# Second-layer weights of four experts kept on chip, in an attention and mixture-of-experts block on one Trainium2 core

## The reference

```python
x = x + tanh(g_xattn[0]) * xattn(layernorm(x), ctx_1024, ...)   # 16 heads of 64, rope on k, clip at 11, softmax over 1024
x = x + tanh(g_ffn[0])   * ffn(layernorm(x), w1, b1, w2, b2, wr, br)

def ffn(x, w1, b1, w2, b2, wr, br):        # 4 experts, w1 256x1024, w2 1024x256, the best 2 for each token
    logits = xf @ wr + br
    topk_vals, topk_idx = top_k(logits, 2)
    gates = softmax(topk_vals)
    h = gelu(einsum('nd,edh->enh', xf, w1) + b1[:, None, :])
    y = einsum('enh,ehd->end', h, w2) + b2[:, None, :]
    c = einsum('eh,ehd->ed', gelu(b1), w2) + b2
    out = sum over the 2 of gates * (y_sel - c_sel + c.sum(axis=0))
```

## Time and profile before

| | |
|---|---|
| median of 3 runs | 1188.68 us (1185.8 to 1188.8) |
| the profiled execution | 1186.63 us |
| its span, first to last instruction | 1184.6 us |
| attention, to the start of the expert phase | about 892 us |
| expert phase, 19 tiles | about 278 us, 892.2 to 1170 |
| last sums and stores | about 15 us |
| mean granted clock | 0.977 |

### The profile page before, as it was taken

The page is one execution under the profiler, slowest core; times in us unless marked ns, Lnnn a source line. Parts: engine busy times, 40 slices in busy tenths (PEclk is TensorE's granted clock), DMA queues, the critical chain, the costliest instruction groups (busy, mean ns, idle before and its releaser), DMA issues.

```text
span 1184.6 us, 22834 instructions
## 1 busy us (share of the span) xinstructions
PE 1084.6 (92%) x7853; PEld 721.2 (61%) x7853; DVE 1049.0 (89%) x1831; ACT 686.5 (58%) x1325; POOL 597.5 (50%) x570
## 2 busy tenths in 40 slices
PE   5799999999899999999999999989789987888995
PEld 3555555655555555655555555646438987888984
DVE  6698999899789999988999988799887889999996
ACT  4555556654455765544566555445356775777772
POOL 6332476343337634333764444247644636665672
PEclk9899999999999999999999999999899999999998
DMA  6100010000000100000000003201218545676654
GB/s 175 35 10 11 19 35 21 10 10 10 12 19 24 32 10 10 10 12 19 24 23 11 19 10 116 77 29 55 91 57 276 194 135 172 206 236 216 226 168 144
DMA packets 74752, 87.89 MB, mean 74 GB/s; under 512 B 11771, under 2 KB 67719, under 8 KB 74632
## 3 DMA queue, kind: packets, MB, share of 16 engines
q1 hardware_dynamic: 71256, 77.82, 21.0%
q0 software_dynamic: 3360, 8.53, 2.0%
q10 hardware_dynamic: 16, 0.00, 0.0%
HBM read 70.57 MB, written 16.54 MB: 74 GB/s over the span
## 4 chain that ended last, share of the span: by engine, by line
PE 62%; DVE 20%; issue 7%; POOL 5%; ACT 4%; DMA 1%; SPq 1%; DVEq 0%; POOLq 0%; ACTq 0%
PE pv L1773 14%; PE sc L1759 13%; PE kv L1704 5%; PE kv L1706 4%; PE kv L1705 4%; DVE acc L1129 4%; PE tr L1745 3%; PE mi L1704 2%; PE mi L1706 2%; PE mi L1705 2%; PE sc L1704 2%; DVE big L1544 2%; PE sc L1706 2%; PE sc L1705 2%; DVE q_hid L1602 2%
## 5 line engine op out<-in xcount | busy, mean ns | idle before, releaser
L899 ACT ACTIVATE prob<-sc 128x1024 f32<-128x1024 f32 x256 | 249.5, 1029 | 223.6 <-PE sc L1759 218.7
L679 POOL TENSOR_TENSOR rot_s<-k_raw,sinb 128x256 f32<-128x256 f32 x128 | 107.3, 839 | 365.7 <-ACT k_raw L845 365.6
L1773 PE MATMUL pv<-prob,val 128*32 128x512 f32 x2048 | 247.7, 601 | 4.6 <-DVE prob L1114 4.6
L1114 DVE TENSOR_SCALAR prob<-prob 128x1024 f32<-128x1024 f32 x256 | 183.0, 728 | 43.4 <-ACT prob L899 36.5
L1759 PE MATMUL sc<-q_hid,big 64*128 64x512 f32 x1536 | 215.1, 412 | 4.7 <-issue 4.7
L1129 DVE TENSOR_TENSOR acc<-acc,prob 128x1024 f32<-128x1024 f32 x128 | 205.2, 1624 | 0.0
L1759 PEld LDWEIGHTS sc<-q_hid,big 64*128 64x128 f32 x1536 | 136.2, 186 | 108.2 <-issue 62.2
L683 POOL TENSOR_TENSOR rot_c<-rot_c,rot_s 128x256 f32<-128x256 f32 x128 | 133.5, 1043 | 45.7 <-DVE rot_c L1103 30.9
L1773 PEld LDWEIGHTS pv<-prob,val 128*32 128x32 f32 x2048 | 56.8, 110 | 115.0 <-issue 90.3
L1704 PE MATMUL sc<-big,q_hid 128*128 128x256 f32 x304 | 92.9, 306 | 30.2 <-DVE q_hid L1602 29.5
L1704 PE MATMUL kv<-big,acts 128*128 128x512 f32 x256 | 115.0, 449 | 5.8 <-DVE rot_c L1103 4.4
(11 more groups left out here) (267 smaller groups left out, 2491.1 us busy)
## 6 DMA issues: line engine op xcount, KB each, us to landing
val<-in_L_ffn_w SPq DMA_DIRECT2D x18, 1024.0 KB, 5.4
prob<-in_L_ffn_w SPq DMA_DIRECT2D x18, 1024.0 KB
slots_x<-lat_r SPq DMA_DIRECT2D x1, 5016.0 KB, 17.9
rows<-slots_x SPq DMA_DIRECT2D x19, 264.0 KB
rows<-in_ctx SPq DMA_DIRECT2D x32, 128.0 KB, 2.1
w_raw<-in_L_xattn_Wq SPq DMA_DIRECT2D x16, 256.0 KB, 2.7
w_raw<-in_L_xattn_Wo SPq DMA_DIRECT2D x64, 64.0 KB
acc<-in_L_ffn_w SPq DMA_DIRECT2D x16, 256.0 KB, 2.7
```

Of the source, the lines that this page charges most:

```text
L679: g.tensor_tensor(rot_s[:].rearrange("p (h a c) -> p h a c", h=4, a=2), kh[:, :, ::-1, :], sinb[:, t].unsqueeze(1).to_broadcast([P, 4, 2, ...
L899: a.activation(prob[:, s % 2, i, :], sc[i][:], ACT.Exp, scale=DH ** -0.5).then_inc(exp_done[i], 1)
L1114: v.tensor_scalar(prob[:, s % 2, i, :], prob[:, s % 2, i, :], EXP_LOW, EXP_HIGH, ALU.max, ALU.min).then_inc(clamped[i], 1)
L1773: last = mm(pv[g * 32:(g + 1) * 32, :], val[:, u % 2, 2 * c + i, at:at + 32], prob[:, s % 2, i, h * N:(h + 1) * N], start=c == 0 and i == ...
```

## The change: what it does, and the diff

1. `w2all` (128 KB for each partition) takes the place of `big`. It holds the split second-layer weights of all four experts. During attention the same memory holds the attention's weights and keys, so the split can begin only in the last unit: ten pieces of 1024 columns (2 of w_1 for tile 0, 8 of w_2) instead of four. POOL makes the low parts of pieces 0, 2, 3, 5, 6 and 8, DVE those of 1, 4, 7 and 9. Three raw buffers are used in turn, the third (`temp`) being DVE's scratch memory for the routing.
2. Each tile fetches only w_1 (1 MB). ACT makes four high parts of 512 columns, at m = 0, 2, 4 and 6, and POOL all four low parts. DVE makes none. One semaphore, `w_low`, is raised after the fourth. The late scatters stand after POOL's second chunk, the scatter of results after the third.
3. PE reads the expert's number itself at the start of each tile (`pe.value_load`) and addresses the second-layer weights by register.
4. The attention loop is written out (a Python `for`), on all engines.
5. The split w_1 of odd tiles lies in pieces of `q_hid`, `wq` and `acts`. The last two of these are read by the attention's last products, so the first low parts for tile 1 wait for `q_mm`, the third for `wo_mm`, the last projection. That projection is moved: both its halves stand at n = 4 (before n = 5 and n = 8), the second half into the bank `tr`. The loads of w_1 for tiles 1 and 2 go to `prob` and wait for the last denominators.

```diff
-        big = [sb(f"big{i}", [4 * KT * 1024], F32R) for i in range(2)]
-        wkv = big[0][:].rearrange("p (l k n) -> p l k n", l=2, k=KT)
-        kst = big[1][:].rearrange("p (u j l s) -> p u j l s", u=2, j=2, l=2)
+        w2all = sb("w2all", [E * 2 * MT * D], F32R)
+        wkv = w2all[:, 0:4 * KT * 1024].rearrange("p (l k n) -> p l k n", l=2, k=KT)
+        kst = w2all[:, 4 * KT * 1024:].rearrange("p (u j l s) -> p u j l s", u=2, j=2, l=2)
...
-        PIECE_AT = (3, 4, 6, 7)
-        PIECES = 4
+        ROUNDS_AT = ((), (), (0, 1), (2,), (3, 4), (5,), (6, 7), (8, 9))
+        POOL_PIECES = (0, 2, 3, 5, 6, 8)
+        DVE_PIECES = (1, 4, 7, 9)
+        PIECES = KT + 2 * E
...
+        def w1_of(job, k, part):
+
+            if job % 2 == 0:
+                return acts[:, (part * KT + k) * 1024:(part * KT + k + 1) * 1024]
+            if part == 0:
+                return q_hid[:, 4 * N + k * 1024:4 * N + (k + 1) * 1024]
+            return (wq[:].rearrange("p l k n -> p (l k n)"), acts[:, 4 * S + 4 * N:4 * S + 4 * N + 1024])[k]
+
+        def w2_of(e, m, part):
+
+            return w2all[:, bass.ds(e * 4096 + (part * MT + m) * D, D)]
...
-            with eng.Fori(0, B - 1) as b:
+            for b in range(B - 1):
...
             def load_piece(piece, e):
 
-                sp.wait_ge(pv_done, (B - 1) * BS + BS - STEPS)
-                wait(sp, p_ready, piece - 1)
+                if piece == 0:
+                    sp.wait_ge(pv_done, (B - 1) * BS + BS - STEPS)
+                if piece == 2:
+                    sp.wait_ge(r_biased, 1)
+                if piece >= 3:
+                    own = POOL_PIECES if piece - 3 in POOL_PIECES else DVE_PIECES
+                    sp.wait_ge(p_lowp if own is POOL_PIECES else p_lowd, own.index(piece - 3) + 1)
...
+                if job < 3:
+                    sp.wait_ge(den_ready, B * PAIRS)
+                else:
+                    sp.wait_ge(w_low, job - 2)
...
+            def w1_low(job, chunk):
+
+                k, cols = chunk // 2, slice(chunk % 2 * 512, (chunk % 2 + 1) * 512)
+                pool.wait_ge(w_high, (job - 1) * 4 + chunk + 1)
+                if job == 1 and chunk == 0:
+                    pool.wait_ge(q_mm, B * PAIRS)
+                if job == 1 and chunk == 2:
+                    pool.wait_ge(wo_mm, B * UNITS * 2)
+                low = g.tensor_tensor(w1_of(job, k, 1)[:, cols], raw_of(job, k)[:, cols],
+                                      w1_of(job, k, 0)[:, cols].bitcast(F32), ALU.subtract)
+                if chunk == 3:
+                    low.then_inc(w_low, 1)
...
             for job in range(1, JOBS):
-                for chunk in pool_lows(job):
-                    w_low(job, chunk)
-                    if chunk == 2:
+                for chunk in range(4):
+                    w1_low(job, chunk)
+                    if chunk == 1:
                         for n in range(*LATE_SCATTERS.get(job, (0, 0))):
                             scatter_late(n)
-                    if chunk == 4 and job > 1:
+                    if chunk == 2 and job > 1:
                         scatter_y(job - 2)
...
-                if job + 1 < JOBS:
-                    w_round(job + 1, m)
+                if job + 1 < JOBS and m % 2 == 0:
+                    w1_round(job + 1, m // 2)
...
+            def piece_low(piece):
+
+                dve.wait_ge(p_high, piece + 1)
+                v.tensor_tensor(piece_of(piece, 1), piece_raw(piece), piece_of(piece, 0).bitcast(F32),
+                                ALU.subtract).then_inc(p_lowd, 1)
...
-                if job + 1 < JOBS:
-                    for chunk in dve_lows(job + 1):
-                        if m == min(chunk + 1, MT - 1):
-                            w_low(job + 1, chunk)
...
             def outputs(n):
 
                 job, m = n // MT, n % MT
                 pe.wait_ge(h_ready, n + 1)
                 if m == 0:
-                    if job:
-                        pe.wait_ge(w_lowp[1], job)
-                        pe.wait_ge(w_lowd[1], job)
                     wait(pe, y_copied, job - 1)
+                    if job in (0, OPEN):
+                        pe.wait_ge(r_owned, 1 + job // OPEN)
+                    expert[0] = pe.value_load(expert_of(job), min_val=0, max_val=E - 1)
                 for i in range(2):
                     last = three(yb[job % 2][:, i * D:(i + 1) * D], lambda l: hid_sp[:, n % 4, l, i * P:(i + 1) * P],
-                                 lambda l: w2v[job % 2][:, l, m, :], m == 0 and i == 0, m == MT - 1 and i == 1,
+                                 lambda l: w2_of(expert[0], m, l), m == 0 and i == 0, m == MT - 1 and i == 1,
                                  skip_group_check=True)
...
-                if n == 5:
+                if n == 4:
+                    pe.wait_ge(s_ready, 2)
                     project(B - 1, UNITS - 1, 0)
-                if n == 8:
-                    pe.wait_ge(wo_out, B * UNITS * 2 - 1)
-                    project(B - 1, UNITS - 1, 1)
+                    project(B - 1, UNITS - 1, 1, tr)
```

More of the change, by code:

```diff
@@ L606, in load_last @@
                     sp.dma_start((rows, more)[r][:, i, 0:D], ys_d[at:at + P, :]).then_inc(ld_z[i], 16)
-            attention(sp, before, step)
+            attention(before, step)
             load_weights(1)
@@ L984, in step @@
                     a.activation(f_tmp[:, 0:EARLY, :], f_logit[:, 0:EARLY, :], ACT.Exp).then_inc(f_exp, 1)
-                if last and u == UNITS - 1 and s in PIECE_AT:
-                    piece_round(PIECE_AT.index(s))
                 if last and i == BS - 1:
                     slots_round(0)
-            attention(act, before, step)
+                if last and u == UNITS - 1:
+                    for piece in ROUNDS_AT[s]:
+                        piece_round(piece)
+            attention(before, step)
             def gelu(n):
@@ L1300, in step @@
                     route_biases()
+                if last and u == UNITS - 1 and s:
+                    for piece in ROUNDS_AT[s - 1]:
+                        if piece in DVE_PIECES:
+                            piece_low(piece)
                 if last and i == BS - 1:
@@ L1534, in slots_low @@
                                 ALU.subtract).then_inc(s_ready, 1)
-            attention(dve, before, step)
-            def w_low(job, chunk):
-                half, c = chunk // 4, chunk % 4
-                cols = slice(c * 512, (c + 1) * 512)
-                dve.wait_ge(w_high[half], (job - 1) * 4 + c + 1)
-                low = v.tensor_tensor(w_of(job, half, 1)[:, cols], raw_of(job, half)[:, cols],
-                                      w_of(job, half, 0)[:, cols].bitcast(F32), ALU.subtract)
-                if chunk == max(n for n in dve_lows(job) if n // 4 == half):
-                    low.then_inc(w_lowd[half], 1)
+            attention(before, step)
             def choose(k):
@@ L1927, in step @@
                     slots_turn(0)
-            attention(pe, before, step)
+            attention(before, step)
             values(B - 1, UNITS - 1, STEPS - 1)
-            w1v = [big[i][:, 0:4096].rearrange("p (l k n) -> p l k n", l=2, k=KT) for i in range(2)]
-            w2v = [big[i][:, 4096:8192].rearrange("p (l m n) -> p l m n", l=2, m=MT) for i in range(2)]
             def hidden(n):
```

173 lines of the change are left out of this document (78 added, 95 removed).

## The result

| | before | changed kernel |
|---|---|---|
| median of 7 runs | 1186.87 us (1185.04 to 1188.80) | 1194.81 us (1192.76 to 1199.74) |
| ratio | | 1.0074, 95% interval 1.0053 to 1.0094 |
| the profiled execution, its span | 1186.63, 1184.6 | 1199.74, 1197.8 |
| mean granted clock of it | 0.977 | 0.968 |
| bytes moved by DMA | 87.89 MB | 72.03 MB |

What follows compares the result with a forecast made beforehand. PE and DVE were taken to bound attention, and DVE, late with low parts PE waits for, the tiles. 1186.63 - 5.3 + 7.4 - 37 + 37 + 0.5 = 1189.2, plus 2.05 to the median: 1191 us, range 1174 to 1203.

Steps and rivals of the forecast that it cites:

- The sign with the largest chance: Whole kernel: slower at 0.41, against faster 0.32 and same 0.27.
- Part 1: Attention loop written out: two jumps back between batches go, -5.3 us, bounds 0 and -7.
- Part 2: Seam between attention and tiles: DVE's four low parts 4.9 us plus one POOL block of 2.55, +7.4 us.
- Piece 0: Seam: POOL's low part of this piece falls into a stretch where DVE waits for the projection.
- First gelu at about 894: Sign of being right at the seam's end: the first gelu at about 894 us, against 892.2 before.
- rival C: Seam: all six POOL pieces hold DVE for their whole 2.55 us; 1198 us, first gelu after 899; chance 0.16.
- Part 3: Tiles: without DVE's 5.1 us of low parts a tile, PE's waits for DVE go, -37 us.
- DVE needs some 9 us of a tile: Tiles: DVE's remaining work per tile; its sign was DVE well under 75% busy in tiles 8 to 13.
- Part 4: Tiles: PE waits for POOL's last w_1 low part behind scatters, 1.35 us a regular tile, 9.5 in tile 5; +37 us.
- Part 5: PE's register loads in the tiles: hidden beside matmuls, +0.5 us, bounds 0 and 9.5.
- rival B: Tiles: PE's register load is not hidden or its matmuls dispatch late, 0.5 us a tile; 1200 us; chance 0.14.
- Rival A: Tiles: POOL's last w_1 chunk is in time, regular tiles lose no 1.35 us; 1172 us; chance 0.22.

Runs made afterwards that it cites:

- E1: Kernel before with its attention loop written out and nothing else changed: 1181.45 us, ratio 0.9958.
- E4: Changed kernel with only four of the ten seam pieces loaded and split, w_2 of experts 1 to 3 left out: 1187.00 us, ratio 1.0007.
- E8: Changed kernel with ACT's first round of tile 1's w_1 behind gelu 1 instead of gelu 0: 1192.43 us, ratio 1.0065.
- E11: Changed kernel with PE loading tile 0's register ahead of its first hidden instead of its first outputs: 1194.02 us, ratio 1.0071.
- E3: Changed kernel with PE loading the register ahead of each of 152 outputs instead of the 19 first ones: 1199.24 us, ratio 1.0106.
- E2: Changed kernel with all of POOL's scatters, late ones included, behind the fourth low part of w_1: 1179.5 us, ratio 0.9943.
- E5: E2 with ACT's rounds of w_1 behind earlier gelus and the late scatters divided differently over the tiles: 1169.47 us, ratio 0.9872.
- E9: Kernel before with E1's loop, w_2 still fetched, all eight low parts of a tile on POOL and none on DVE: 1243.57 us, ratio 1.0469.
- E7: Kernel before with E1's loop, w_2 still fetched, six instead of five of eight low parts on POOL: 1210.41 us, ratio 1.0211.
- E10: E5 with DVE's last two w_2 pieces moved into tile 0 and PE's first register load ahead of its first hidden: 1166.68 us, ratio 0.9824.

## Why the prediction was right or wrong

The sign with the largest chance (slower, 0.41) and the range held. The point did not: it said no change, +2.6 us, and the change is +7.9. The measured time is 3.5 us above the forecast's 1191.3, the change 5.3 us, because the median of the kernel before came out 1.8 us lower than the one the forecast had. Step by step:

- **Part 1, -5.3:** right in size, E1 gives -5.0. The two gaps of PE went as said; that 2.8 us of them would come back as waits for DVE's rows was not foreseen, and what made up for it is open.
- **Part 2, +7.4:** the size was right (7.1 and 7.2 in two traces, 7.8 by E4), its parts were not, and that is luck: POOL's pieces cost DVE 6.6 us more than before instead of 2.55 (some 4.3 in E8), and DVE's own four 4.8 as forecast. DVE had more room than said: 2.9 us vanished in its waits for ACT and PE. Piece 0, said to fall where DVE waits, held a pair of clamps for 2.2 us. "First gelu at about 894": 894.56 in E8; 901.69 in the profiled execution, which was already 7.2 us behind E8's at the start of the last unit; rival C's threshold of 899 was set without room for that. Rival C's mechanism came close all the same (six pieces held DVE, for 12.3 us of its 15.3); its time did not, since E4 gives 7.8 us where C meant 11 or more.
- **Part 3, -37:** right in what it named, DVE's waits gone. One thing said there was wrong: "DVE needs some 9 us of a tile", under 75% busy. Window of tiles 8 to 13, changed kernel:

```profile
1032.00:1113.90 81.90, 74.50 (x602) 73.46 (x601) 71.48 (x127) 51.80 (x110) 42.77 (x36) 0.98 0.46 152
```

  That is 87%, 11.9 us a tile: the steps of the constants rose from 700 to 1074 ns on average, held by POOL's parts, and of the 4.6 us a tile that DVE's low parts had taken before, only 1.9 left its busy time (13.8 us a tile before). It did not matter, because PE's 11.96 us are longer still.
- **Part 4, +37:** right as a sum. By distances between starts of PE's weight loads over 0.3 us, less a cadence, tiles 0 to 18 have 39.3 us of gaps before and 40.7 after. A regular tile lost 1.39 (1.35 forecast), tile 5 6.3 for POOL (9.5), tiles 6 and 7 3.7 and 2.0 (3.5, 2.2), tile 0 2.3 (2.0). Tile 5 was priced as if DVE's own waits of 3.4 us there had gone; they stayed, and with them the sum.
- **Part 5, +0.5:** near. 18 loads lie under matmuls, the first is exposed and takes 0.9 us (E11); rival B's price of 0.5 us a load is refuted by E3.
- **What was missing** is in tiles 0 and 1. The forecast gave them 3.4 us of new waits, which against the 2.2 us of gaps that went there is +1.2; they cost 5.6 in the profiled execution, 3.6 in E8. In the last 14 us ahead of the first gelu the starts of PE's weight loads are 2.4, 1.0, 2.0, 0.9, 2.2, 3.2 and 1.8 us apart in seven places (before 3.3, 2.7, 1.1 and 1.0 in four), and then its clock is 0.71 in the first 12.9 us of the tiles, 0.89 in E8, and was 1.00; the changed kernel, then E8, then before:

```profile
901.70:914.60 12.90, 12.02 (x76) 11.73 (x76) 8.30 (x21) 8.05 (x17) 3.02 (x2) 0.71 0.52 195
```

```profile
894.60:907.50 12.90, 12.02 (x92) 11.73 (x91) 8.71 (x22) 8.94 (x19) 3.09 (x2) 0.89 0.55 208
```

```profile
892.20:905.10 12.90, 11.89 (x97) 11.50 (x97) 10.94 (x23) 11.56 (x25) 7.29 (x5) 1.00 1.01 347
```

  No term of the sum was for the clock. My reading is that a change that turns work into waits of PE pays for each wait, and in some executions again behind it: the seven runs lie between 1192.76 us at a clock of 0.975 and 1199.74 at 0.968, while the kernel before has 0.976 to 0.979 in most of its runs. How much of the 5.3 us this explains is open. No run here held the clock fixed, the three runs at 0.975 took 1192.76 to 1194.81 us, all above the forecast, and a run of the kernel before with a clock of 0.930 took only 1191.84. By E8's trace 2.4 us of the miss lie in tiles 0 and 1.

Rival A named the right lever with the wrong outcome: POOL was not in time, and gains of the size it promised (19 us) came only when the order on POOL was changed (15.3 us in E2, 25.3 in E5).

## What to carry to other kernels

When work is taken off the engine that others wait for, write down for each remaining producer the moment at which its last piece is wanted and what stands ahead of it in its queue; scatters in front of the last low part (2.4 us in a regular tile, 3.6 more where three late ones were added) undid the whole gain, though POOL was half idle, and moving them, with ACT's rounds earlier, was worth 25 us. Do not balance DVE and POOL by counts of instructions: here, where both read two tensors of SBUF, DVE was held for as long as POOL's row of parts lasted. And compare single executions only where their granted clock is alike.

## What the runs showed of the hardware that I had not expected

- A DVE instruction with two SBUF inputs is held not by one POOL instruction but by a row of them: 7.01 us for one of 0.48 (E9), 4.93 for one of 0.67 (E7). The Trainium skill (SBUF — State Buffer, "Who interferes with whom") has whoever issues first hold the shared ports "for the whole instruction" (said there of the two-port modes; of two SBUF inputs it says that they contend). The trace of E9 shows DVE blocked over five POOL instructions in a row. Which of the two comes second cannot be read from the starts: in the changed kernel the first of the two instructions below starts 0.52 us ahead of POOL's part (1057.90), beside a scatter, and is still held (2.10 us). Beside a scatter with no part behind it, in E10 at 1047.95, it keeps its usual 0.48 us.

```profile
1057.38 2.62 DVE L1583 SCALAR_TENSOR_TENSOR recip<-acc,gb,recip 128x256 f32<-128x256 f32 x2
```

- PE's load of a register takes 0.30 us and costs 0.03 us where matmuls are queued ahead, 0.9 us where PE had run empty. Register-addressed matmuls kept the cadence of 0.12 us.
- The same code behind the same wait of 3.0 us ran at a granted clock of 1.00 in one execution and 0.50 in another.
